# Windowed attention with a spiking feed-forward on 8 cores: the second product moved ahead of the scores within a step

## The reference, cut to what matters

```python
g = (LN(x) @ Wg.T + bg)  split in 16 heads of 64
v = (LN(x) @ Wv.T + bv)  split in 16 heads of 64
corr = g_i . g_j / (|g_i| |g_j|)             # 2048 x 2048 per head
corr = (corr * m + 1) / 2                    # m: j <= i and j >= i - 128
denom = mean_j(corr) + 0.5
fitness = 1 / (denom * sum_i(1 / denom))     # one number per row, a sum over all rows of the head
attn = softmax(corr * fitness on m, -1e10 elsewhere)
x = x + (attn @ v) @ Wo.T + bo
h = relu(LN(x) @ W_fc.T) ** 2                # 4096 wide
x = x + mean of 5 spikes of (h @ W_proj.T)
```

## Time and profile before

| | us |
|---|---|
| median of the runs (1677.83 and 1679.36) | 1678.6 |
| the profiled execution | 1678.2 |
| its span, on core 3, the slowest | 1676.3 |
| spans of the other cores | 1666.5 to 1675.7 |
| PE busy (matmuls) | 1028.7 |
| DVE busy | 689.7 |
| ACT busy | 667.8 |

### The profile page before, as it was taken

One profiled execution on the slowest core, in us unless ns is written; L12 is line 12 of the kernel. 1 busy time (PEld: TensorE's weight loads), 2 busy tenths in 40 slices (PEclk: granted clock), 3 DMA queues, 4 the chain that ended last, 5 costly groups with the idle time before them and its releaser, 6 DMA issues.

```text
span 1676.3 us, 16533 instructions; the slowest of 8 cores (1666.5 to 1676.3 us)
## 1 busy us (share of the span) xinstructions
PE 1028.7 (61%) x4632; PEld 433.5 (26%) x4632; DVE 689.7 (41%) x1639; ACT 667.8 (40%) x1467; POOL 130.4 (8%) x216
## 2 busy tenths in 40 slices
PE   0024555594566665666656887888687868887700
PEld 0022222241222222222222333333233323333300
DVE  1300222200555655555543012089306960494098
ACT  1354332331466666666664542064304540351000
POOL 1011221111000000000000100110011101111100
PEclk9999787797555555555557998999799989999955
DMA  9987665454000000000004344433534444455301
GB/s 183 223 182 135 100 101 103 110 109 107 11 1 1 1 1 1 1 1 1 1 1 139 101 126 138 138 126 126 185 121 139 136 160 140 130 159 175 101 29 47
DMA packets 78908, 158.69 MB, mean 95 GB/s; under 512 B 38627, under 2 KB 38884, under 8 KB 78820
## 3 DMA queue, kind: packets, MB, share of 16 engines
q0 software_dynamic: 63824, 106.97, 26.8%
q1 hardware_dynamic: 14996, 50.68, 9.1%
HBM read 147.15 MB, written 33.55 MB: 108 GB/s over the span
## 4 chain that ended last, share of the span: by engine, by line
DMA 29%; PE 25%; DVE 18%; issue 11%; ACT 10%; another core or an unknown queue 4%; POOL 1%; DVEq 1%; ACTq 0%; POOLq 0%; SPq 0%
PE psY L834 9%; DMA wpb<-wprojC 7%; DMA wstg<-wfcT 6%; PE psY L796 5%; DMA wstg<-wprojT 5%; ACT ebf L526 4%; DMA wfcb<-wfcC 4%; ACT PT L585 4%; DMA wfcC<-wstg 3%; DVE memb L873 3%; DVE t1b L870 3%; DMA wprojC<-wstg 3%; PE psPV L599 3%; PE psPT L577 2%
## 5 line engine op out<-in xcount | busy, mean ns | idle before, releaser
L796 PE MATMUL psY<-x2nT,wfcb 128*128 128x512 bf16 x1024 | 242.7, 396 | 50.7 <-DMA wfcb<-wfcC 49.6
L834 PE MATMUL psY<-wpb,h_sb 128*128 128x512 bf16 x1024 | 234.5, 386 | 38.4 <-DMA wpb<-wprojC 37.8
L599 PE MATMUL psPV<-PT,v_sb 128*64 128x128 bf16 x512 | 104.1, 307 | 98.4 <-ACT PT L585 98.4
L526 ACT ACTIVATE ebf<-C,fit 128x256 f32<-128x256 f32 x256 | 151.3, 591 | 2.3 <-DVE em L565 0.6
L796 PEld LDWEIGHTS psY<-x2nT,wfcb 128*128 128x128 bf16 x1024 | 101.0, 101 | 191.7 <-issue 90.7
L834 PEld LDWEIGHTS psY<-wpb,h_sb 128*128 128x128 bf16 x1024 | 98.4, 99 | 173.1 <-issue 68.4
L577 PE MATMUL psPT<-ident_sb,em 128*128 128x128 bf16 x512 | 98.0, 295 | 56.4 <-DVE em L565 56.4
L805 ACT ACTIVATE frb<-psY 128x512 f32<-128x512 f32 x128 | 76.6, 599 | 121.6 <-PE psY L796 121.4
L862 DVE TENSOR_SCALAR spkA<-y 128x1024 f32<-128x1024 f32 x16 | 11.1, 694 | 270.0 <-ACT y L852 268.7
L852 ACT ACTIVATE y<-psY 128x512 f32<-128x512 f32 x32 | 16.1, 628 | 263.1 <-PE psY L834 263.1
L478 PE MATMUL psD<-g_sb 64*128 64x256 bf16 x256 | 99.2, 390 | 30.7 <-DMA wprojC<-wstg 27.0
(11 more groups left out here) (99 smaller groups left out, 1223.0 us busy)
## 6 DMA issues: line engine op xcount, KB each, us to landing
wfcb<-wfcC POOLq DMA_DIRECT2D x64, 512.0 KB, 4.3
wpb<-wprojC POOLq DMA_DIRECT2D x64, 512.0 KB, 3.9
xa<-xin SPq DMA_DIRECT2D x32, 512.0 KB, 5.0
wstg<-wfcT POOLq DMA_DIRECT2D x32, 256.0 KB, 5.4
xpair<-xin SPq DMA_DIRECT2D x8, 1024.0 KB, 12.3
wfcC<-wstg POOLq DMA_DIRECT2D x16, 512.0 KB, 3.4
wstg<-wprojT POOLq DMA_DIRECT2D x16, 512.0 KB, 5.4
wprojC<-wstg POOLq DMA_DIRECT2D x16, 512.0 KB, 2.9
```

Of the source, the lines that this page charges most:

```text
L526: e = b.op("S", lambda h, hb=hb, qt=qt, q4=q4: h.activation(ebf[q4][:], C_sb[hb][:, 256 * qt:256 * qt + 256], AF.Exp, scale=fitb[hb][:, qt ...
L599: mpv = b.op("T", lambda h, h_i=h_i, hp=hp, qt=qt, q4=q4, pb=pb, half=half: h.matmul(psPV[pb][hp:hp + 64, 128 * (q4 % 2):128 * (q4 % 2) + ...
L796: mmt = b.op("T", lambda h, f=f, fp=fp, k=k, gi=gi: h.matmul(psY[f % 2][:], wfcb[fp % 2][:, 1024 * (f % 2) + 128 * k:1024 * (f % 2) + 128 ...
L834: last = b.op("T", lambda h, f=f, f2=f2, tti=tti, nh=nh, pj=pj: h.matmul(psY[pj][:], h_sb[:, 512 * f + 128 * tti:512 * f + 128 * tti + 128 ...
```

## The change

In a step of the pipeline `emit_pv` is now called ahead of `emit_pass1`. No instruction is added or taken away.

```diff
--- before.py
+++ after.py
@@ -619,10 +619,10 @@
     def hq(j):
         return j // NT, j % NT
     for i in range(NSTEP + 23):
+        if i >= 22 and i - 22 < NSTEP:
+            emit_pv(*hq(i - 22))
         if i < NSTEP:
             emit_pass1(*hq(i))
-        if i >= 22 and i - 22 < NSTEP:
-            emit_pv(*hq(i - 22))
         if i >= 17 and i - 17 < NSTEP:
             emit_e(*hq(i - 17))
             if (i - 17) % NT % 2 == 1:
```

## The result

The changed kernel takes 1705.96 us in the median, the one before, in ten runs, 1679.83 us. The ratio is 1.015, with a 95% interval of 1.0117 to 1.0184: slower, by 1.5%. It is taken from the fast runs alone: in some executions, of either kernel, one half of the chip runs at a lower granted clock and takes longer, and these are left out of every ratio here, but not of the medians. Forecast were 1702.8 us and 1.4%.

What follows compares the result with a forecast made beforehand. The attention stage was taken as bound by a ring of waits. Even heads 7 x 2.36, odd heads 7 x 0.88 and 1.5 for head 14 gave 24.2 us: 1678.6 + 24.2 = 1702.8 us, range 1692 to 1712.

Steps and rivals of the forecast that it cites:

- The bound: Attention stage: held by a ring of waits, not a full engine; copy to copy 3.17 us in even heads, 3.44 odd.
- The ring over the exponential: Named in a follow-up's forecast: copy, exponential ebf, s_sb, em, odd step's PT, next copy; 2.82 us per two steps.
- ring A: Copy, waiting PV, three more PE slots, x1T, exponential, next copy: 3.17 us even heads, 3.44 odd, length kept.
- Ring B: Newly closed by the change: copy, waiting PV, psD, C, s_sb, em, odd step's PT, copy: 3.41 us.
- Even heads +0.24, odd heads +0: Added us per regular pair (two loop steps, copy to copy): even max(3.17, 3.41), odd max(3.44, 3.41).
- The statistics: Once per head, the copy-to-copy interval with the statistics chain grows: 5.13 to 5.48 us even, 4.87 to 5.45 odd.
- The interval after it: Copy-to-copy interval following the statistics, with two s_sb instructions: 3.74 us, +0.57 in even heads, +0.30 in odd.
- The sum: Over 117 pairs, heads 0 to 13 and five pairs of head 14: 16.5 + 6.2 + 1.5 = 24.2 us.
- Rival 1: psD starts although the PV ahead of it waits; not slower, 1678.6 us; chance 0.06.
- Rival 2: psD's weights load while PV waits or runs, slot 0.22; half the loss, 1691.5 us; chance 0.10.
- rival 3: psD behind PV costs 0.15 more in both rings; slower by over 2%, 1718.3 us; chance 0.12.
- The doubt at its end: Forecast fails if the parity effect comes from phase between ACT and its neighbours, not the head; no size given.

Runs made afterwards that it cites:

- one slot more: PV ahead of psD in even steps only, against the kernel before: ratio 1.0238, 1732.0 us.
- one fewer: PV ahead of psD in odd steps only, against the kernel before: ratio 0.987, 1668.5 us.
- no wait at PV: PV two steps later, against the kernel before: ratio 0.9803 with psD first, 0.9764 with PV first.
- Two different cuts on DVE: On top of the whole change, C behind em: ratio 1.0035; or em ahead of s_sb in even steps: 0.9995. Both ratios against the kernel before.

## Why the prediction was right

- **The bound.** That the stage is held by a ring from copy to copy through four PE slots is shown, not only argued: one slot more gave 3.49 and 3.77, one fewer 2.84 and 3.13, and no wait at PV 2.83. (The ring over the exponential is 2.83 too, so with one slot fewer it is the odd heads that show ring A.)
- **Ring B, 3.41 us.** Each of its seven steps came out in the trace after within 0.01 us, the unseen slot of psD behind PV among them: 0.33. Two different cuts on DVE took it away.
- **Even heads +0.24, odd heads +0.** 3.17 to 3.41, and 3.44 to 3.45.
- **The statistics.** 5.13 to 5.49 in an even head, forecast 5.48, and in four of seven odd ones 4.87 to between 5.43 and 5.49, forecast 5.45 (the other three had another length before and grew by 0.47 to 0.58); psD's later place cost nothing there. The interval after it is 3.72 or 3.73 in 12 of 14 heads, forecast 3.74.
- **The sum.** 24.2 us forecast, 25.2 measured over the stage. (The median is 3.2 us above the 1702.8 forecast; 1.2 of that is the base, 1679.8 in ten runs and not 1678.6.) The step that fell short is "Odd heads: ... +0". It holds for most regular pairs, but with almost no spare time left on DVE's side, single late starts now lengthen a pair, and the forecast didn't count them. The last pair of the 14th head shows one that was there before, hidden. Before, on DVE and ACT:

```profile
831.78 0.60 ACT L585 ACTIVATE PT<-psPT 128x512 bf16<-128x512 f32 x1
...
833.45 0.17 DVE L554 RECIPROCAL rqb<-s_sb 128x2 f32<-128x2 f32 x1
...
833.84 0.48 DVE L565 SCALAR_TENSOR_TENSOR em<-ebf,rqb,maskA_sb 128x256 bf16<-128x256 f32 x1 [0.22 <-issue]
...
835.22 0.60 ACT L585 ACTIVATE PT<-psPT 128x512 bf16<-128x512 f32 x1
```

and after:

```profile
855.00 0.60 ACT L585 ACTIVATE PT<-psPT 128x512 bf16<-128x512 f32 x1 [0.30 <-PE psPT L577]
...
857.25 0.17 DVE L554 RECIPROCAL rqb<-s_sb 128x2 f32<-128x2 f32 x1
857.65 0.48 DVE L565 SCALAR_TENSOR_TENSOR em<-ebf,rqb,maskA_sb 128x256 bf16<-128x256 f32 x1 [0.24 <-issue]
...
858.75 0.60 ACT L585 ACTIVATE PT<-psPT 128x512 bf16<-128x512 f32 x1 [0.32 <-PE psPT L577]
```

In both, em starts 0.39 to 0.40 behind the reciprocal, where 0.09 is usual, with nothing that it waits for. Before, the interval was 3.44 all the same; now it is 3.75, 0.31 over the forecast. Three more pairs are as much too long in the trace after, at the same places on all eight cores: one by 0.31 (C at 485.24 came 0.85 behind psD and not 0.50), one by 0.24 (the copy at 559.49 started 0.26 late on ACT), and one of an even head by 0.21 beyond its 0.24 (s_sb at 827.11 came 0.57 behind C and not 0.35). The four make 1.07 us; what is left of the difference nearly cancels.
- **The rivals.** Rival 1 (psD overtakes the waiting PV) would have left 3.17; C waited 149.3 us for psD instead, and psD never started less than 0.32 behind the PV ahead of it. Rival 2 (a slot of 0.22) and rival 3 (0.48) are out by the slot of 0.33. The Trainium skill's rule that a change of tiling mode drains the engine ("TensorEngine Tiling (Array Packing)", Key Properties) goes with that slot: the new neighbours have as many mode changes as the old, and cost the same. How long such a drain is by itself no run here shows.
- **The doubt at its end,** that the parity effect might be one of phase, was unfounded: it followed the partitions of PV and x1T.

## What to carry to other kernels

In a software pipeline on queues that run in order, find the wait that closes the ring and count what stands between it and the next instruction that the ring needs; work without a wait of its own belongs ahead of the waiting instruction, or behind the last one that the ring needs. Taking psD out from between the two PVs was worth 0.31 to 0.33 us per pair here, and taking C or s_sb out from ahead of em the 0.24 per pair of an even head that the change had cost. An edit that moves the same two calls in every step can be two edits of opposite sign, so try the parities apart. Where a tile is consumed right after it is made, one more pair of distance (two steps later here, with no more buffers) can be worth more than a better order: 2.0 to 2.4% here, and the best order alone 1.3%.

## What the runs showed of the hardware that I had not expected

- An ACT instruction over 64 partitions (x1T) costs the instructions behind it more when its operands lie on partitions 64 to 127. The pair took 3.44 us with PV, psPV, bias and output there, 3.30 with bias and output or either one, and 3.17 with none. In the traces the exponential starts 0.49 behind x1T and not 0.37 when bias or output is high, and with psPV high too the copy starts 0.72 behind that exponential and not 0.58 to 0.60. Why is open.
- On DVE, single instructions start about 0.3 us late at fixed places of the program with nothing to wait for. Two em 0.38 to 0.40 behind the reciprocal (usual: 0.08) and a reciprocal 0.67 to 0.69 behind s_sb (usual: 0.32) are the same three instructions in the kernels before and after and in all eight others that keep DVE's order, on all eight cores; they stand 218 and 219 of the timeline's DVE instructions apart. The four kernels with another DVE order don't have them there. A ring with spare time hides them and one without shows them. What they are was not tried.
